# An expert stage of sixteen wide and seven narrow slots, in place of nineteen and four

## What is computed

```python
gate_logits = x_flat @ gate_w.T                       # 2048 x 8
topk_vals, topk_idx = jax.lax.top_k(gate_logits, 2)
topk_w = jax.nn.softmax(topk_vals, axis=-1)
comb = comb.at[jnp.arange(T)[:, None], topk_idx].add(topk_w)
for e in range(8):
    h = jax.nn.gelu(x_flat @ w1[e].T + b1[e], approximate=False)   # 256 -> 1024
    y = h @ w2[e].T + b2[e]                                        # 1024 -> 256
    out = out + comb[:, e:e + 1] * y
```

## Time and profile before

| | |
|---|---|
| time, three runs | 1119.06, 1123.71, 1127.06 us (median 1123.71) |
| span of the profiled execution | 1127.1 us |
| TensorE matmuls busy | 967.3 us, 86% |
| ScalarE, VectorE, GpSimd busy | 748.1, 675.2, 577.1 us |
| expert stage, from the first load of rows (869.8 us) | 257 us |
| of it TensorE busy from 876 us to 1112 us | all but some 2 us |

### The profile page before, as it was taken

One profiled execution on the slowest core, in us unless ns is written; L12 is line 12 of the kernel. 1 busy time (PEld: TensorE's weight loads), 2 busy tenths in 40 slices (PEclk: granted clock), 3 DMA queues, 4 the chain that ended last, 5 costly groups with the idle time before them and its releaser, 6 DMA issues. The chain is left out here.

```text
span 1127.1 us, 21116 instructions
## 1 busy us (share of the span) xinstructions
PE 967.3 (86%) x6828; PEld 587.3 (52%) x6828; DVE 675.2 (60%) x1963; ACT 748.1 (66%) x949; POOL 577.1 (51%) x474
## 2 busy tenths in 40 slices
PE   2962489989999999998999998798940999999994
PEld 1631144434444444443444454456740898998983
DVE  6833677777777877777777753654643343443431
ACT  4521389979999999998999984654320645555551
POOL 6503469886777777776755874200354122323231
PEclk9985589989999999999999998999965999999998
DMA  6498564574436635457256325850542123323233
GB/s 196 104 282 271 183 188 148 197 261 139 171 120 232 244 112 181 158 194 248 97 184 213 117 92 205 313 207 25 201 166 75 45 45 59 53 46 59 36 46 93
DMA packets 74012, 169.27 MB, mean 150 GB/s; under 512 B 13490, under 2 KB 43058, under 8 KB 68210
## 3 DMA queue, kind: packets, MB, share of 16 engines
q1 hardware_dynamic: 49634, 98.41, 26.4%
q0 software_dynamic: 20416, 68.32, 20.3%
q10 hardware_dynamic: 3856, 1.19, 0.5%
HBM read 121.65 MB, written 62.36 MB: 163 GB/s over the span
## 5 line engine op out<-in xcount | busy, mean ns | idle before, releaser
L1023 DVE CUSTOM_DVE_ANT_0 masked<-ps,maskA 128x512 f32<-128x512 f32 x512 | 347.2, 689 | 120.5 <-PE ps L1452 117.6
L1452 PE MATMUL ps<-ks,qs 96*128 96x512 f32 x512 | 261.4, 550 | 53.6 <-DMA qs<-q_low 27.8
L1339 ACT ACTIVATE masked<-masked,negmax 128x2048 f32<-128x2048 f32 x128 | 256.3, 2003 | 69.1 <-DVE negmax L1029 68.5
L1400 ACT ACTIVATE weights<-ps 128x1024 f32<-128x1024 f32 x256 | 253.8, 1014 | 37.6 <-PE ps L1475 35.1
L1473 PE MATMUL ps<-qs,ks 98*128 98x512 f32 x512 | 230.5, 509 | 3.7 <-DMA qs<-shift_lo 3.7
L1475 PE MATMUL ps<-maskB,identb 128*128 128x512 bf16 x512 | 202.6, 396 | 0.0
L1452 PEld LDWEIGHTS ps<-ks,qs 96*128 96x128 f32 x512 | 102.3, 200 | 141.1 <-DVE piecemax L1023 95.2
L1722 POOL DMA_INDIRECT sum_rows<-y,ids x42 | 65.2, 1552 | 179.8 <-DVE y L1760 160.2
L1487 PE MATMUL ps<-weights,v_all 128*32 128x256 f32 x2048 | 138.0, 387 | 0.9 <-ACT weights L1400 0.9
L1742 DVE TENSOR_TENSOR gT<-ffn_w,gT 128x2048 f16<-128x2048 f32 (+1 forms) x23 | 48.5, 2107 | 133.0 <-ACT gT L1799 133.0
L842 POOL TENSOR_SCALAR wch<-wch 128x1024 f32<-128x1024 f32 x36 | 100.3, 2786 | 36.3 <-DMA wch<-in_L_gnn_W 32.2
(11 more groups left out here) (188 smaller groups left out, 1124.2 us busy)
## 6 DMA issues: line engine op xcount, KB each, us to landing
expert_rows<-pad_rows POOLq DMA_DIRECT2D x73, 272.0 KB, 6.0
split_weights<-whl POOLq DMA_DIRECT2D x36, 512.0 KB, 3.2
adjA<-in_adj SPq DMA_DIRECT2D x16, 1024.0 KB, 8.1
adjB<-in_adjT SPq DMA_DIRECT2D x32, 512.0 KB, 6.7
wall<-split_weights SPq DMA_DIRECT2D x16, 1024.0 KB, 15.1
wch<-in_w1T POOLq DMA_DIRECT2D x16, 512.0 KB, 6.2
wch<-in_w2T POOLq DMA_DIRECT2D x16, 512.0 KB, 6.2
xr<-expert_rows SPq DMA_DIRECT2D x19, 272.0 KB, 2.9
```

Source lines behind the costliest of these rows:

```text
L1023: dve.tensor_tensor_reduce(masked[:, a % 2, k * 512:(k + 1) * 512], ps[:, u % 2, :], maskA[:, a, k * 512:(k + 1) * 512], 1.0, NO_EDGE, ALU ...
L1339: act.activation(masked[:, a % 2, :], masked[:, a % 2, :], ACT.Exp, bias=negmax[:, h % 2, a:a + 1], accum_out=rowsum[:, h % 4, a:a + 1]).t ...
L1400: act.activation(weights[:, j % 4, :, :], ps[:, 2 + 2 * (j % 2):4 + 2 * (j % 2), :], ACT.Exp).then_inc(weights_ready, 1)
L1452: pe.matmul(ps[:, u % 2, :], qs[0:KR, h % 4, a * P:(a + 1) * P], ks[0:KR, h, k * 512:(k + 1) * 512], start=True, stop=True)\
```

## The change

The 39 blocks are cut into 16 wide slots and 7 narrow ones: `NPAIR` is 4096 / 256 = 16, `NHALF` is 39 − 32 = 7, and `SLOTS` is 23 as before. There can be more than sixteen pairs (up to nineteen). A pair beyond the sixteenth is taken by two narrow slots, which are given the same pair and row offsets 0 and 128. For this two constant rows are written on GpSimd, `pair_of` (the pair that a slot would take: 0 to 15, then 16, 16, 17, 17, ...) and `half_at` (0, or 0 and 128 in turn), and the table is computed from `turn` (a slot's place in the order of pairs and singles) in place of `blocks`.

```diff
--- before.py
+++ after.py
@@ -67,8 +67,10 @@
         inv_rows = dram("inv_rows", [NB * H + 1, TB], F32)
         TOPK = 2
         PR = 2 * P
-        NPAIR = (TOPK * T // P + E - 1) // 2
-        SLOTS = TOPK * T // PR + E - 1
+        HALVES = TOPK * T // P + E - 1
+        NPAIR = TOPK * T // PR
+        NHALF = HALVES - 2 * NPAIR
+        SLOTS = NPAIR + NHALF
         REGION = T + PR
         ROW = 272
         SETS = E + 1
@@ -547,7 +549,8 @@
             return at(name, shape, dt, where)
 
         past = at("past", [P, 3, SLOTS, 2 * E], F32, M_ADJA + 8 * KB)
-        tabf = small("tabf", [P, 7, SLOTS], F32, 1)
+        tabf = small("tabf", [P, 12, SLOTS], F32, 1)
+        spare = small("spare", [P, 1], F32, 1)
         group = small("group", [P, 5, 3 * E], F32, 1)
         base = small("base", [P, 4 * E + 1], F32, 1)
         b1s = small("b1s", [P, E, HC], F32, 1)
@@ -573,6 +576,8 @@
         region0 = small("region0", [P, E], F32, 0)
         tokens = small("tokens", [P, NT], F32, 0)
         blocks = small("blocks", [P, SLOTS], F32, 0)
+        pair_of = small("pair_of", [P, SLOTS + NHALF % 2], F32, 0)
+        half_at = small("half_at", [P, SLOTS + NHALF % 2], F32, 0)
         before = small("before", [P, P], BF16, 0)
         onesb = small("onesb", [P, P], BF16, 0)
         nblk = small("nblk", [P, 3, E], F32, 0)
@@ -942,7 +947,15 @@
                 pool.memset(onesb[:, :], 1.0).then_inc(c3_ready, 1)
                 for q in range(2):
                     pool.memset(rows[:, q, :, D + E:ROW], 0.0).then_inc(c3_ready, 1)
-                pool.wait_ge(c3_ready, 7)
+                half_pairs = (NHALF + 1) // 2
+                pool.iota(pair_of[:, 0:NPAIR], pattern=[[1, NPAIR]], base=0, channel_multiplier=0,
+                          allow_small_or_imprecise_dtypes=True).then_inc(c3_ready, 1)
+                pool.iota(pair_of[:, NPAIR:NPAIR + 2 * half_pairs], pattern=[[1, half_pairs], [0, 2]], base=NPAIR,
+                          channel_multiplier=0, allow_small_or_imprecise_dtypes=True).then_inc(c3_ready, 1)
+                pool.memset(half_at[:, 0:NPAIR], 0.0).then_inc(c3_ready, 1)
+                pool.iota(half_at[:, NPAIR:NPAIR + 2 * half_pairs], pattern=[[0, half_pairs], [P, 2]], base=0,
+                          channel_multiplier=0, allow_small_or_imprecise_dtypes=True).then_inc(c3_ready, 1)
+                pool.wait_ge(c3_ready, 11)
                 pool.affine_select(out=before[:, :], in_=onesb[:, :], compare_op=ALU.is_gt, fill=0.0, base=0,
                                    pattern=[[1, P]], channel_multiplier=-1).then_inc(c3_ready, 1)
                 row_factors(0, 3)
@@ -1237,7 +1250,7 @@
                         attention_sum(3)
                 attention_moments(3)
                 scale_shift(2)
-                dve.wait_ge(c3_ready, 8)
+                dve.wait_ge(c3_ready, 12)
                 dve.tensor_copy(place[:, :], region0[:, :]).then_inc(rank_read, 1)
                 for f in range(FC):
                     split_hidden(1, f)
@@ -1292,7 +1305,7 @@
                 choose_second(3)
                 send(3)
 
-                dve.wait_ge(c3_ready, 11)
+                dve.wait_ge(c3_ready, 15)
                 cnt = nblk[:, 0, :]
                 then(dve.tensor_tensor(cnt, place[:, :], region0[:, :], ALU.subtract))
                 then(dve.tensor_scalar(nblk[:, 1, :], cnt, float(P - 1), None, ALU.add))
@@ -1312,14 +1325,27 @@
                                            group[:, i, E - reach:E + G2 - reach], ALU.add))
                 ends = group[:, 4, E:E + G2]
                 then(dve.tensor_tensor(base[:, G2 + 1:2 * G2 + 1], base[:, 1:G2 + 1], base[:, 0:G2], ALU.subtract))
-                then(dve.tensor_tensor(past[:, 0, :, :], blocks[:, :].unsqueeze(2).to_broadcast([P, SLOTS, G2]),
+
+
+
+                pairs = group[:, 4, G2 - 1:G2]
+                mark(dve.tensor_scalar(tabf[:, 7, :], pair_of[:, 0:SLOTS], pairs, None, ALU.is_lt))
+                then(dve.tensor_scalar(spare[:, :], pairs, -float(NPAIR), 0.0, ALU.add, ALU.max))
+                mark(dve.tensor_tensor(tabf[:, 11, :], tabf[:, 7, :], half_at[:, 0:SLOTS], ALU.mult))
+                then(dve.tensor_scalar(tabf[:, 8, :], blocks[:, :], spare[:, 0:1], None, ALU.subtract))
+                then(dve.tensor_tensor(tabf[:, 9, :], pair_of[:, 0:SLOTS], tabf[:, 8, :], ALU.subtract))
+                then(dve.tensor_tensor(tabf[:, 9, :], tabf[:, 9, :], tabf[:, 7, :], ALU.mult))
+                then(dve.tensor_tensor(tabf[:, 10, :], tabf[:, 9, :], tabf[:, 8, :], ALU.add))
+                turn = tabf[:, 10, :]
+                then(dve.tensor_tensor(past[:, 0, :, :], turn.unsqueeze(2).to_broadcast([P, SLOTS, G2]),
                                        ends.unsqueeze(1).to_broadcast([P, SLOTS, G2]), ALU.is_ge))
                 mark(dve.tensor_tensor(past[:, 1, :, :], past[:, 0, :, :],
                                        group[:, 0, E:E + G2].unsqueeze(1).to_broadcast([P, SLOTS, G2]), ALU.mult))
                 then(dve.tensor_tensor(past[:, 2, :, :], past[:, 0, :, :],
                                        base[:, G2 + 1:2 * G2 + 1].unsqueeze(1).to_broadcast([P, SLOTS, G2]), ALU.mult))
                 then(dve.tensor_reduce(tabf[:, 0:3, :], past[:, :, :, :], AX.X, ALU.add))
-                mark(dve.tensor_tensor(tabf[:, 3, :], blocks[:, :], tabf[:, 1, :], ALU.subtract))
+                mark(dve.tensor_tensor(tabf[:, 3, :], turn, tabf[:, 1, :], ALU.subtract))
+                mark(dve.tensor_tensor(tabf[:, 2, :], tabf[:, 2, :], tabf[:, 11, :], ALU.add))
                 then(dve.tensor_scalar(tabf[:, 4, :], tabf[:, 0, :], float(E), -float(E), ALU.is_ge, ALU.mult))
                 mark(dve.scalar_tensor_tensor(out=tabf[:, 5, :], in0=tabf[:, 3, :], scalar=float(PR),
                                               in1=tabf[:, 2, :], op0=ALU.mult, op1=ALU.add))
@@ -1633,7 +1659,7 @@
                 for f in range(FC):
                     hidden(3, f)
                     if f == 4:
-                        pe.wait_ge(c3_ready, 8)
+                        pe.wait_ge(c3_ready, 12)
                         ranks(0)
                 back(2, 0)
                 turn_xn(1)
```

## The result

The changed kernel takes 1110.76 us (median of 4 runs, 1107.75 to 1113.41), the kernel before in the same comparison 1121.38 us (1118.83 to 1127.06). The ratio is 0.9896, with a 95% interval from 0.9863 to 0.9929: 1.04% faster, where 0.94% and 1113.2 us were forecast. The kernel is clearly faster; whether by more than 1% the interval leaves open. The forecast of 1113.2 us started from a median of before of 1123.71 us; with its fourth run, 1118.83, that median is 1121.38, and this accounts for 2.3 of the 2.4 us between forecast and time.

What follows compares the result with a forecast made beforehand. TensorE was taken to bound the expert stage, its queue setting the sustained narrow pace. Iterations 14 to 19 fall from 58.3 to 47.8 us, all else hidden: 1123.71 less 10.55 gives 1113.2 us, range 1109 to 1117.5.

Steps and rivals of the forecast that it cites:

- What bounds the kernel: Expert stage: TensorE's pieces lie end to end from slot 15 on, so time saved there shortens the run.
- The price of the slots: Iterations 14 to 19 on TensorE: 58.3 us before, 47.8 us after narrowing slots 16 to 18, a gain of 10.55 us.
- The choice of 7.40 over 6.14: Iterations 17 to 19: each priced at the sustained 7.40 us set by TensorE's queue, not 6.14, which would gain 14.3 us.
- Rival one: Iterations 17 to 19: narrow ones run at TensorE's own pace, 6.14 us; gain 14.3 us, time 1109.4; chance 0.12.
- the account of the lead: First narrow iteration: TensorE's queue is still ahead from wide work, so it costs 6.14 us once, then 7.40.
- The table and the constants: Ahead of the stage: at most 1.6 us more on VectorE and 0.7 on GpSimd, both hidden by waits, costed at nothing.
- rival two: Narrow iterations: row loads land late, up to 1 us lost in each of four; gain about 6.5, time 1117; chance 0.10.
- rival three: Narrow slots: waits for scatter landings become the bound, about 1129 us at landings of 10 us; chance 0.03.
- The profiled execution: The profile of before: its 1127.1 us span was taken as that of the slowest of the three runs shown.

Runs made afterwards that it cites:

- experiment 2: The changed kernel run again, unchanged: 1112.48 us, ratio to the kernel before 0.9895.
- (5): Changed kernel with the slot number loaded two more times per iteration in TensorE's queue, no more work for the engine: 1122.30 us.
- experiment 6: Changed kernel with expert fixed to 0 on TensorE in the seven narrow slots, so no addresses or slot numbers there; the choice of weights is left out: 1101.75 us.
- (1): Changed kernel with its seven narrow slots placed among the wide ones by a permutation: 1105.36 us, ratio to the kernel before 0.9859.
- (7): Changed kernel cut into 4 wide and 31 narrow slots instead of 16 and 7: 1158.02 us.
- (4): The changed kernel's constants and table code, but with 19 wide and 4 narrow slots, so the table alone: 1117.33 us.
- 8: Changed kernel with 18 wide and 5 narrow slots, so one slot narrowed instead of three: 1118.41 us.
- 3: The kernel before run again, unchanged, for a second profile: 1119.40 us.

## Why the prediction was right

**What bounds the kernel.** Right. TensorE's pieces follow one another in the chain of after as in the earlier trace rows.

**The price of the slots.** Right in each iteration to 0.14 us: 47.6 us measured, 47.8 forecast, a gain of 10.7 us for 10.55. That the medians of the runs differ by 10.6 us, so near to it, is in part luck: the interval of the ratio is some 7 us wide, and against the same kernel experiment 2 gave 8.9. The forecast leaned slightly to a result within 1%; the measured 1.04% is 0.1 point beyond the forecast 0.94%, and both lie in the interval (0.7% to 1.4%).

**The choice of 7.40 over 6.14.** Right, and for the reason given. That the queue's pace sets the sustained narrow iteration is shown from four sides: work added to the queue alone lengthens it (5), work taken from the queue alone shortens it (6), an order in which wide slots rebuild the lead removes it at unchanged work (1), and it holds over 28 iterations, most of them far from the end (7). Rival one is excluded by 7 and 1: narrow slots one behind another are slow in the middle of the stage too, and near its end they are fast behind wide ones.

**What was off in that step** is the account of the lead. The prediction took 6.14 us for the engine's own pace. Without computed addresses the engine needed 5.52 (6), so 6.14 was already partly the queue's. This did not touch the sum, which took 6.14 as it was measured. The Trainium skill ("TensorE: Matmul & The Clock Gate", section "Back-to-back issue gap") has N/2.4 + 2.5 for the isolated gap, some 56 ns at 128 columns; the trace of 6 agrees with that figure, in a stream of 48 in 2.68 us. The same section's sustained 81 ns lies between what the runs show with address computations in between, some 65 ns on a lead and 87 to 91 ns without, and none shows 81.

**The table and the constants.** Right. On VectorE the piece from the last `base` operation to the end of the table took 5.75 us (846.19 to 851.94) for 4.06 before (851.15 to 855.21), 1.7 us more for the 1.6 estimated, and hidden (4). The other 0.3 of the 2.0 us lies ahead of the table: GpSimd's last row of eight scatters starts 0.3 us sooner relative to VectorE, in the profiles of after and of experiments 1, 2, 4 and 8 alike; why is open. 11.7 us of cover are left.

**Late rows, rival two.** Did not happen. TensorE waits for no rows in iterations 14 to 22 of after. The load for slot 19, and its time to landing:

```profile
1051.90 0.34 SPq L1719 DMA_DIRECT2D xr<-expert_rows  x1
...
DMA to landing us min/median/max: 2.1/2.1/2.1
```

The rows landed at 1054.0, and their transposes are in the chain from 1055.47: a slack of some 1.4 us, within the 0.7 to 1.6 of the prediction. In experiment 6, where the narrow iterations take 5.5 us, the load for the same slot took 3.04 us and landed at 1053.00, 0.08 us after the second half before had ended (1052.92 in the timeline); the transposes started at 1053.05. With such a landing after would have had some 0.5 us left. What made that one longer is open.

**The chain of scatters, rival three.** Did not happen, in 31 narrow slots either (7). In the tail it costs what the prediction read from the earlier trace rows: the last two scatters of after are 4.58 us apart, for 4.67.

**The profiled execution.** The prediction took the span of 1127.1 us for that of the slowest run shown, 1127.06 us. In all profiles since, the time of a run is 1.7 to 1.8 us more than its span, so that profile was probably of a run of its own, of about 1128.8 us. The gain does not depend on it, but a comparison of the two profiles by their spans would have given 15.4 us, half as much again as the 10.6 us between the medians.

## What to carry to other kernels

When a stage is cut into finer pieces, read the price of a piece from where such pieces follow each other for long, not from the first of them: the first may be paid by a lead that the sequencer built up during longer work. The queue's records (here the address computations) beside the engine's show which of the two sets the pace. Pieces that are bound by the queue cost less placed between pieces that are bound by the engine: here another order gave 6.3 us in the stage without any work saved, and that version had the lowest median of the study among those that compute everything.

## What the runs showed that I had not expected

A matmul of 128 columns at a granted clock of 1.00 (2.4 GHz) cost 56 ns where its queue computes no addresses and loads no slot number, 63 to 67 ns with 32 computed addresses for 48 matmuls on a lead, and 87 to 91 ns with them and no lead. Even the narrow second half, 24 matmuls of 256 columns, took 2.81 us or more with the queue in step, and 2.62 without address computations (6) or behind a wide first half (1). And the part ahead of GpSimd's constants, which no edit touched, ended at moments 12 us apart in the ten profiles, while the expert stage repeated to 0.1 us (2 and 3). What moves it is open; TensorE's first matmul alone starts between 16.1 and 18.4 us.
